# ScalarE copies the down weights of an expert tile, and gathered token rows have eight places

## The reference

```
x = x + 0.5 * moe(layernorm(x))
x = x + mamba(layernorm(x)) + mamba(flip(layernorm(x)))     # two state space layers, 16 states
x = x + 0.5 * moe(layernorm(x))                             # the same weights again
moe:  logits = x @ gate_w.T ; top 2 of 8 experts, softmax of the two
      out = sum over the two experts e of  p_e * ((silu(x @ wg_e.T) * (x @ wu_e.T)) @ wd_e.T)
```

## Time and profile before

| what | us |
|---|---|
| median of 3 runs | 2813.0 |
| span of the profiled execution, first to last instruction | 2637.8 |
| median less the span | 175.2 |
| POOL busy | 2198.0 (83%) |
| PE busy | 2244.2 (85%) |
| VectorE busy | 2254.8 (85%) |
| ScalarE busy | 1909.6 (72%) |
| first gather to last scatter, pass 0 | 104.34 to 495.59 |
| first gather to last scatter, pass 1 | 2203.30 to 2593.81 |

### The profile page before, as it was taken

One profiled execution on the slowest core, in us unless ns is written; L12 is line 12 of the kernel. 1 busy time (PEld: TensorE's weight loads), 2 busy tenths in 40 slices (PEclk: granted clock), 3 DMA queues, 4 the chain that ended last, 5 costly groups with the idle time before them and its releaser, 6 DMA issues.

```text
span 2637.8 us, 49017 instructions
## 1 busy us (share of the span) xinstructions
PE 2244.2 (85%) x15840; PEld 1920.7 (73%) x15840; DVE 2254.8 (85%) x3430; ACT 1909.6 (72%) x3628; POOL 2198.0 (83%) x1402
## 2 busy tenths in 40 slices
PE   4899999768888898898898898988988768999992
PEld 3799999547676677777777676766777647999982
DVE  8766666789999999999999999999999897666666
ACT  4355555378998998998999899999898544555551
POOL 3577777369999999999999999999999936777771
PEclk8899999889999999999999999999999878999996
DMA  7011111433333333333333333333333240111116
GB/s 247 17 48 50 49 49 49 121 107 104 105 109 106 109 102 101 106 107 100 109 103 102 110 103 105 110 106 106 105 102 111 76 160 25 49 50 49 49 50 204
DMA packets 156813, 248.60 MB, mean 94 GB/s; under 512 B 22082, under 2 KB 66018, under 8 KB 155874
## 3 DMA queue, kind: packets, MB, share of 16 engines
q1 hardware_dynamic: 137568, 202.79, 25.9%
q0 software_dynamic: 18208, 37.26, 5.2%
q10 hardware_dynamic: 866, 6.43, 0.6%
HBM read 213.10 MB, written 33.29 MB: 93 GB/s over the span
## 4 chain that ended last, share of the span: by engine, by line
POOL 28%; PE 23%; issue 22%; DVE 14%; ACT 8%; DMA 4%; POOLq 0%; ACTq 0%; DVEq 0%; SPq 0%
POOL buf L484 10%; POOL buf L545 9%; DVE buf L914 6%; PE bank L1544 6%; POOL token_outputs L494 5%; PE bank L1419 4%; DMA buf<-state_rows 3%; PE bank L1329 3%; PE bank L1519 3%; POOL buf L532 2%; DVE buf L901 2%; ACT scaled L1194 2%; ACT over L1161 2%; DVE bank L886 2%; PE bank L1348 2%
## 5 line engine op out<-in xcount | busy, mean ns | idle before, releaser
L545 POOL TENSOR_TENSOR buf<-buf 128x1024 f32<-128x1024 f32 x512 | 1199.9, 2378 | 33.8 <-PE bank L1544 28.9
L914 DVE TENSOR_TENSOR_SCAN buf<-over,bank 128x512 f32<-128x512 f32 x832 | 953.6, 1198 | 5.2 <-PE bank L1519 2.6
L1161 ACT ACTIVATE over<-wgu,negA 128x510 f32<-128x510 f32 x832 | 541.2, 710 | 39.6 <-DVE buf L914 28.5
L1544 PE MATMUL bank<-id_sb,buf 128*128 128x128 f32 x4096 | 521.8, 282 | 6.3 <-POOL buf L545 6.3
L1544 PEld LDWEIGHTS bank<-id_sb,buf 128*128 128x128 f32 x4096 | 483.9, 146 | 55.8 <-issue 46.5
L1348 PE MATMUL bank<-parts 128*128 128x256 f32 x3408 | 480.3, 291 | 3.3 <-DVE buf L764 1.9
L1348 PEld LDWEIGHTS bank<-parts 128*128 128x128 f32 x3408 | 428.8, 192 | 7.2 <-issue 4.1
L1194 ACT ACTIVATE scaled<-wd_sb,I 128x256 f32<-128x256 f32 x896 | 377.3, 498 | 22.3 <-PE bank L1519 22.2
L494 POOL DMA_INDIRECT token_outputs<-buf,slot_out x284 | 287.7, 1013 | 111.1 <-issue 83.2
L484 POOL DMA_INDIRECT buf<-token_rows,slot_token x284 | 297.1, 1046 | 95.4 <-issue 89.7
L1519 PE MATMUL bank<-id_sb,scaled 128*128 128x128 f32 x1792 | 257.2, 281 | 91.3 <-ACT scaled L1194 40.8
(11 more groups left out here) (170 smaller groups left out, 2978.0 us busy)
## 6 DMA issues: line engine op xcount, KB each, us to landing
buf<-state_rows SPq DMA_DIRECT2D x608, 256.0 KB, 3.2
token_rows<-buf SPq DMA_DIRECT2D x32, 256.0 KB, 2.3
wd_sb<-token_outputs SPq DMA_DIRECT2D x16, 512.0 KB, 4.1
buf<-token_outputs SPq DMA_DIRECT2D x16, 512.0 KB, 4.9
buf<-token_rows,slot_token POOLq DMA_INDIRECT x284, 2.6
token_outputs<-buf,slot_out POOLq DMA_INDIRECT x284, 2.3
out<-X SPq DMA_DIRECT2D x16, 256.0 KB, 3.8
wgu<-wgT ACTq DMA_DIRECT2D x1, 2048.0 KB, 8.1
```

Of the source, the lines that this page charges most:

```text
L545: pool.tensor_tensor(hC[:, b, :].rearrange("p (c w) -> p c w", c=C), hs[:, b, :].rearrange("p (c w) -> p c w", c=C), Cs[:, b, :].unsqueeze ...
L914: V.tensor_tensor_scan(hs[:, b, w], dA[:, b, c, :, :].rearrange("p s t -> p (s t)"), source, 0.0, ALU.mult, ALU.add).then_inc(s[f"scan_don ...
L1161: ins = A.activation(dA[:, n % R, c, :, 1:], delta[r][:, c * W:(c + 1) * W].rearrange("p (s t) -> p s t", s=S)[:, :, 1:], ACT.Exp, scale=n ...
L1544: ins = M.matmul(bank[4 + q // 2][:, at:at + P], hC[:, n % R, c * W + q * P:c * W + (q + 1) * P], id_sb[:, :], is_transpose=True, start=Fa ...
```

## The change

VectorE no longer copies the down weights: its `low_w` ends with the second subtraction, which now raises `wlo_dve`. ScalarE has a new function `down_w`, with the same wait for `down_pe`, which copies them by an activation and raises a new semaphore `wd_act`. It stands behind silu of half 0 of the preceding tile, ahead of `copy_out` and silu of half 1; that of tile 0 stands behind `high_w(0)`. PE's `down` waits for `wd_act` besides.

The gathered rows get eight places (X_BUFS = 8) and eight semaphores instead of four. They lie at another part of the same buffer. POOL gathers tiles 0 to 7 ahead, then for each i gather(i+8), scatter(i). PE's loop is written over eight tiles: tiles 0 to 7 unrolled, 7 turns of eight, 7 more tiles. `yo`, `wd_e` and the loops of ACT and DVE keep four.

```diff
+X_BUFS = 8
-        xin = carve(0, 4 * HT * D).rearrange("p (b h d) -> p b h d", h=HT, d=D)
+        xin = carve(8192, X_BUFS * HT * D).rearrange("p (b h d) -> p b h d", h=HT, d=D)
                 def get_tokens(i):
-                    wait(pool, s["turned_pe"], m * TILES + i - 3)
+                    wait(pool, s["turned_pe"], m * TILES + i + 1 - X_BUFS)
...
-                for i in range(4):
+                for i in range(X_BUFS):
                     get_tokens(i)
                 for i in range(TILES):
-                    if i + 4 < TILES:
-                        get_tokens(i + 4)
+                    if i + X_BUFS < TILES:
+                        get_tokens(i + X_BUFS)
                     put_outputs(i)
...
-                def low_w(i, q, e):
+                def low_w(i, b, e):
...
-                    wait(dve, s["down_pe"], m * TILES + i - 3)
-                    V.tensor_copy(wd_e[:, q, :].rearrange("p (c d) -> p c d", d=D),
-                                  wd_sb[:, bass.ds(e * IC, IC), :]).then_inc(s["wlo_dve"], 1)
+                    ins.then_inc(s["wlo_dve"], 1)
...
+                def down_w(i, q, e):
+
+                    wait(act, s["down_pe"], m * TILES + i - 3)
+                    A.activation(wd_e[:, q, :].rearrange("p (c d) -> p c d", d=D),
+                                 wd_sb[:, bass.ds(e * IC, IC), :], ACT.Copy).then_inc(s["wd_act"], 1)
...
                         silu(i, 0)
+                        if more:
+                            down_w(i + 1, (q + 1) % 4, e)
...
                 def turn_slots(i, q, k):
-                    pe.wait_ge(s[f"xin{q}"], (m * USES[q] + k + 1) * HT * DMA)
+                    pe.wait_ge(s[f"xin{q}"], (m * X_USES[q] + k + 1) * HT * DMA)
...
                 def down(i, b, q):
                     pe.wait_ge(s["hid_dve"], 2 * (m * TILES + i) + 2)
+                    pe.wait_ge(s["wd_act"], m * TILES + i + 1)
...
-                def four(k, count=4):
+                def eight(k, count=X_BUFS):
...
-                four(0)
-                with pe.Fori(1, LOOPS) as k:
-                    four(k)
-                four(LOOPS, LAST)
+                eight(0)
+                with pe.Fori(1, X_LOOPS) as k:
+                    eight(k)
+                eight(X_LOOPS, X_LAST)
```

More of the change, by code:

```diff
@@ L150, in macaron_kernel @@
     USES = [len(range(b, TILES, 4)) for b in range(4)]
-    assert LAST
+    X_USES = [len(range(b, TILES, X_BUFS)) for b in range(X_BUFS)]
+    X_LOOPS, X_LAST = TILES // X_BUFS, TILES % X_BUFS
+    assert LAST and X_LAST
     assert D == P and C == 2 and I == 512 and W == 512 and NG == NP and NG % 2 == 0
@@ L310, in macaron_kernel @@
             logit_done logits_act route_dve route_pe route_act xin0 xin1 xin2
-            xin3 st0 st1 st2 st3 turned_pe xhi_act xlo_dve whi_act wlo_dve gate_pe up_pe
+            xin3 xin4 xin5 xin6 xin7 st0 st1 st2 st3 turned_pe xhi_act xlo_dve whi_act wlo_dve wd_act gate_pe up_pe
             silu_act hid_dve down_pe yo_act comb_done comb_first stored diff_done mask_done slots_done
@@ L484, in get_tokens @@
                         pool.indirect_dma_start(
-                            out=xin[:, i % 4, h, :], out_offset=None, in_=xn_rows[:, :],
+                            out=xin[:, i % X_BUFS, h, :], out_offset=None, in_=xn_rows[:, :],
                             in_offset=bass.IndirectOffsetOnAxis(ap=slot_token[:, i * HT + h:i * HT + h + 1], axis=0)
-                        ).then_inc(s[f"xin{i % 4}"], DMA)
+                        ).then_inc(s[f"xin{i % X_BUFS}"], DMA)
                 def put_outputs(i):
@@ L760, in low_w @@
                     for k, w in ((0, wg_sb), (1, wu_sb)):
-                        V.tensor_tensor(w_lo[:, q % 2, k * I:(k + 1) * I], w[:, bass.ds(e * I, I)],
-                                        w_hi[:, q % 2, k * I:(k + 1) * I].bitcast(F32), ALU.subtract)
-                    wait(dve, s["down_pe"], m * TILES + i - 3)
-                    V.tensor_copy(wd_e[:, q, :].rearrange("p (c d) -> p c d", d=D),
-                                  wd_sb[:, bass.ds(e * IC, IC), :]).then_inc(s["wlo_dve"], 1)
+                        ins = V.tensor_tensor(w_lo[:, b, k * I:(k + 1) * I], w[:, bass.ds(e * I, I)],
+                                              w_hi[:, b, k * I:(k + 1) * I].bitcast(F32), ALU.subtract)
+                    ins.then_inc(s["wlo_dve"], 1)
                 def hidden(i, b, h):
@@ L783, in four @@
                         if more:
-                            low_w(i + 1, (q + 1) % 4, e)
+                            low_w(i + 1, (q + 1) % 2, e)
                         hidden(i, q % 2, 0)
@@ L1079, in moe @@
                 high_x(0, 0)
-                high_w(0, 0, expert_of(0))
+                first = expert_of(0)
+                high_w(0, 0, first)
+                down_w(0, 0, first)
                 four(0)
@@ L1372, in down @@
                     ins.then_inc(s["down_pe"], 1)
-                def four(k, count=4):
+                def eight(k, count=X_BUFS):
                     for q in range(count):
-                        i = k * 4 + q
+                        i = k * X_BUFS + q
                         if not (isinstance(i, int) and i == TILES - 1):
-                            turn_slots(i + 1, (q + 1) % 4, k + 1 if q == 3 else k)
+                            turn_slots(i + 1, (q + 1) % X_BUFS, k + 1 if q == X_BUFS - 1 else k)
                         gate(i, q % 2, 0)
```

## The result

The changed kernel takes 2838.99 us (median of 4 runs, 2835.44 to 2842.81); beside it the kernel before takes 2813.95 us (2808.58 to 2816.86). The ratio is 1.0088, 95% interval 1.0075 to 1.0101: slower by 25 us, where 10.6 us faster was forecast.

What follows compares the result with a forecast made beforehand. POOL, at 5.355 us a tile against PE's 4.87, was taken to bound the expert passes. Gains of 5.4 and 5.2 us, copy and loop 0, sum to 10.6 us off the 2813.0 us median: 2802 us, range 2776 to 2816.

Steps and rivals of the forecast that it cites:

- the copy: Expert passes: 142 down-weight copies moved to ScalarE, at most 0.60 us each, fit into its waiting; effect 0, bounds 0 and 0.
- the places: Expert passes: eight places for gathered rows let POOL gather further ahead; all of the forecast 10.6 us gain comes from here.
- pause of 6.72 us filled: Start of pass: POOL issues 16 gathers, not 8, before the first tile's output, filling its 6.72 us idle time ahead of 123.50.
- sixteen gathers done: Start of pass: 16 gathers at 1.28 us, 20.4 us, plus one delay of 0.4 put POOL at 125.2 us.
- 63 steps of gather and scatter: Middle of pass: 22 steps at 5.48 us (120.6 us), then 41 at 5.40 us (221.4 us), ending at 467.2.
- end behind them: End of pass: only scatters remain and PE is late; 23.0 us against 16.06 now, so the pass ends at 490.2.
- hold in the locked rhythm: From about tile 22: VectorE's two-SBUF-input subtraction, running when a second scatter starts, lengthens that POOL instruction by 0.25 us.
- gain of the passes: Two expert passes: the first ends at 490.2 instead of 495.6, 5.4 us earlier; the second gains 5.2 us.
- PE's loop of eight tiles: PE's longer loop body, 7 turns: possible reload of 0 to 3.8 us a turn, within PE's 4.2 us slack; taken as 0.
- A: Expert passes: VectorE's copy is what delays POOL's DMAs, so all delays vanish; each pass 23.3 us earlier, 2766 us; chance 10%.
- B: Locked tiles: the subtraction starts after the scatter's start and delays it only 0.05 us; 8.2 us more gained per pass, 2786; 16%.
- C: Locked tiles: the subtraction starts just before the scatter, delaying it 0.5 us; tiles cost 5.65 us, 10.3 us more a pass, 2822; 14%.

## Why the prediction was wrong, step by step

**The step that failed** is in the sum: "the median of the runs, 2813.0, lies 175.2 above that, in which nothing changes". The 175.2 us were taken to lie around the span. They lie in the expert passes, nearly all of them as one wait of 3 us in every second tile, and both edits change what happens there. So two terms of the sum didn't hold where the time was taken: the copy, "0, bounds 0 and 0", measured +17 us (1.0066), and the places, 10.6 us off, measured +9.5 us (1.0032). With it fell "POOL waits for nobody and sets the pace": true of the profile shown, not of the timed runs. Nothing in the rows showed what 175 us around the span could be, and in every later profiled run only 2 us lie there. A second reading, that the profile and the times are of different conditions, was not among the rivals.

**The mechanism, where its premise holds** (faster kind, pass 0):

| step | worked out | measured |
|---|---|---|
| pause of 6.72 us filled | yes | yes |
| sixteen gathers done | 125.2 | 125.90, two of them held by 0.5 us |
| 63 steps of gather and scatter | 342.0 us | 469.92 - 125.90 = 344.0 us |
| end behind them | 23.0 us | 492.82 - 469.92 = 22.9 us |
| hold in the locked rhythm | 0.25 us, second scatters | 1.17 to 1.47 us long in turn, against 0.98: 0.29 us in the mean |
| gain of the passes | 5.4 and 5.2 us | 3.0 and 3.3 us |
| copy | 0 | 1.0000 |
| PE's loop of eight tiles | 0 | 0.9998 |
| gain of the whole | 10.6 us | 6.4 us |

The mechanism was right there and the holds were mis-sized: the 63 steps took 344.0 - 63 x 5.15 = 19.6 us more than undisturbed ones, where the sum had 22 x 0.33 + 41 x 0.25 = 17.5. Twice these 2.0 us are the missing 4 us. All gathers and scatters of the pass together are held 22.1 us instead of 13.8. With places alone one pass had 21.4 us of holds and lasted 387.5 us, the other had 15.8 and lasted 381.2, and that kernel gains 12.7 us. So in the combination the copy is not quite free (0.9976 against 0.9951). That it acts by the phase at which the subtraction meets GpSimd is argued from these two passes, not shown.

**Of the rivals**, A fell with the copy alone. B and C were both about the phase of the lock. C had the sign of the result, 2822 us, but that is no hit of C: on the slower kind another wait sets the pace. A premise that all cases shared was wrong, and so the range of 2776 to 2816 didn't hold 2839.

**On the slower kind**, shown: the places cost some 10 us at the start of a pass and give 7 back at its end; the copy costs 0.16 us a tile, nearly as much behind the second silu; the loop costs nothing; without most of the gathers the lateness is gone. Argued only: that the copy costs because ScalarE has its whole turn to do once a late signal arrives (in the rows at 314.15 silu, copy and copy-out follow each other without a pause). Not settled: by what way the gathers delay TensorE's signals, why only on some chips, and why fewer held DMAs make the wait longer. No kernel that computes all and was run beats the kernel before on both kinds. The eight places without the copy are the best on the faster kind (-0.49%) and cost 0.32% on the slower.

## What to carry to other kernels

Before a trace is used for a sum, compare the profiled execution's span with the timed runs: a gap of more than the few microseconds around the span means that the trace shows another bound than the one that is timed, and every "hidden" in it is in doubt. Then measure the unchanged kernel again with a profile, beside the change. An engine that looks free of waits in one trace can be the one that waits on another chip, so an edit that only feeds it earlier, or lends another engine's slack, should be priced on both.

## What the runs showed of the hardware

- The same program takes 2637 to 2638 us on two chips and 2794 to 2814 us on three; without most of its indirect gathers it takes 2575 and 2580 us.
- On the slower three, semaphore increments of TensorE come late in the passes with indirect gathers (185 of 333 by more than 0.3 us, a tenth by over 4.4 us), and its products go out singly for stretches, 0.72 us apart, in some of the kernels. The granted clock does not explain it: 0.97 in the stretch of the kernel before, 1.00 in that of the loop of eight tiles, which took as long as the kernel before on its chip (0.9998).
- An indirect DMA of GpSimd is stretched by up to 0.5 us by a subtraction with two SBUF inputs that runs at its start, and not by one whose second input is in PSUM (those that start inside it: 0.98 us against 1.24 in the mean; all scatters: 990 ns against 1066).
